# Layer 1 of a four-layer graph network: a second whole weight block, edge passes spread among the moments, column terms moved to GpSimd and ScalarE

## What is computed

```python
h = x @ W;  s1 = h @ a1;  s2 = h @ a2
e = leaky_relu(s1[:, :, None] + s2[:, None, :], 0.2)
att = softmax(where(adj > 0, e, -9e15), axis=1)      # over i, for each column j
x = layernorm(x + elu(att @ h))
```

## Time and profile before

| what | value |
|---|---|
| median of three runs | 418.67 us |
| profiled execution, its own time | 419.3 us |
| its span in the profile | 417.1 us |
| TensorE, weight load, VectorE busy | 362.8, 321.0, 363.4 us |
| ScalarE, GpSimd busy | 307.5, 296.0 us |
| TensorE clock granted, mean | 0.974 of full |

### The profile page before, as it was taken

The page is one execution under the profiler, slowest core; times in us unless marked ns, Lnnn a source line. Parts: engine busy times, 40 slices in busy tenths (PEclk is TensorE's granted clock), DMA queues, the critical chain, the costliest instruction groups (busy, mean ns, idle before and its releaser), DMA issues. The chain is left out here.

```text
span 417.1 us, 9207 instructions
## 1 busy us (share of the span) xinstructions
PE 362.8 (87%) x2786; PEld 321.0 (77%) x2793; DVE 363.4 (87%) x1398; ACT 307.5 (74%) x824; POOL 296.0 (71%) x363
## 2 busy tenths in 40 slices
PE   7898999999969687796896899999998789899980
PEld 7697999999968686796796889899898685455550
DVE  0558899999999999999999988899998997899984
ACT  2757999999766767758858867678786737888862
POOL 5347888777776775664765767777777856899994
PEclk9999999999989999989989999999999989999996
DMA  6999963000000000000000000000000000012222
GB/s 174 217 250 247 244 108 53 2 1 2 2 1 2 1 2 1 2 2 1 2 1 2 2 0 2 2 1 2 0 2 3 0 2 1 2 75 79 75 77 105
DMA packets 8756, 18.20 MB, mean 44 GB/s; under 512 B 1280, under 2 KB 2560, under 8 KB 8704
## 3 DMA queue, kind: packets, MB, share of 16 engines
q0 software_dynamic: 2304, 8.39, 10.6%
q1 hardware_dynamic: 5280, 8.72, 5.9%
q10 hardware_dynamic: 1120, 0.46, 0.5%
HBM read 21.76 MB, written 4.19 MB: 62 GB/s over the span
## 5 line engine op out<-in xcount | busy, mean ns | idle before, releaser
L542 PE MATMUL o_ps<-h_scaled,PT 128*128 128x129 f32 (+1 forms) x1536 | 186.8, 281 | 2.8 <-DVE y L1085 1.2
L542 PEld LDWEIGHTS o_ps<-h_scaled,PT 128*128 128x128 f32 x1536 | 181.4, 197 | 4.8 <-issue 2.5
L1029 DVE SCALAR_TENSOR_TENSOR PT<-rows_ps,factors,MT 128x512 f32<-128x512 f32 x128 | 88.8, 738 | 0.0
L781 ACT ACTIVATE X<-y,rstd 128x128 f32<-128x128 f32 x192 | 61.2, 391 | 28.1 <-POOL rstd L304 28.1
L304 POOL TENSOR_TENSOR rstd<-var_eps,neg_half 128x4 f32<-128x4 f32 x64 | 70.1, 1095 | 5.0
L479 PE MATMUL h_ps<-wx,xT 128*128 128x130 f32 x384 | 53.5, 283 | 20.9 <-DVE smax L978 19.0
L479 PEld LDWEIGHTS h_ps<-wx,xT 128*128 128x128 f32 x384 | 48.4, 194 | 26.6 <-issue 26.4
L1105 DVE BATCH_NORM_STATS2 stats<-y 128x6 f32<-128x128 f32 x256 | 55.9, 281 | 6.5 <-DVE y L1085 0.5
L254 POOL TENSOR_TENSOR mean_term<-h_mean,empty_row 128x512 f32<-128x512 f32 x32 | 38.2, 1194 | 18.7 <-DVE residual L1085 14.1
L319 POOL TENSOR_TENSOR elu_exp<-elu_exp,X 128x512 f32<-128x512 f32 x32 | 40.8, 1275 | 7.8 <-ACT elu_exp L774 7.4
L278 POOL TENSOR_TENSOR h_scaled<-hx,factors 128x516 f32<-128x516 f32 x32 | 35.1, 1097 | 13.5 <-PE o_ps L542 7.9
(11 more groups left out here) (120 smaller groups left out, 650.7 us busy)
## 6 DMA issues: line engine op xcount, KB each, us to landing
MT<-adj_by_j POOLq DMA_DIRECT2D x16, 512.0 KB, 13.0
X<-x SPq DMA_DIRECT2D x16, 256.0 KB, 8.3
out<-X SPq DMA_DIRECT2D x16, 256.0 KB, 2.0
w_rel<-w SPq DMA_DIRECT2D x1, 256.0 KB, 3.5
w_back<-w_by_output ACTq DMA_DIRECT2D x1, 192.0 KB, 3.2
wx<-w_by_input ACTq DMA_DIRECT2D x1, 192.0 KB, 3.6
bias<-b ACTq DMA_DIRECT2D x1, 64.0 KB, 3.0
bias<-b SPq DMA_DIRECT2D x1, 64.0 KB, 5.9
```

Source lines behind the costliest of these rows:

```text
L542: last = pe.matmul(o_ps[it.b][:, ic, first:1 + D], PT[:, it.b, jc, ic * P:(ic + 1) * P], h_scaled[:, it.b, jc, first:1 + D], start=(jc == ...
L781: last = act.activation(X[:, it.g, c, :], y[:, it.b, c, :], ACT.Copy, scale=rstd[:, it.b, c:c + 1])
L1029: dve.scalar_tensor_tensor(out=PT[:, it.b, c, :], in0=rows_ps[:], scalar=factors[:, it.b, 1, c:c + 1], in1=m, op0=ALU.max, op1=ALU.mult, * ...
```

## The change

Of the four blocks two are whole instead of one (`WHOLE = 2`), so GpSimd makes two mask-times-rows passes per item, ScalarE fills two blocks, and VectorE makes two edge passes and two masking passes instead of three and three. BELOW is computed on GpSimd, ABOVE on ScalarE as a ReLU with the maximum as bias, and the column weight on GpSimd, as a sum instead of a maximum. take_max(n+3) stands ahead of the column sums. From slot 17 to slot 29 the edge passes of item n+2 are made in slot n, one between sum and moments and one between moments and aggregate, in place of those of item n+1 at the head of the next slot.

```diff
-WHOLE = 1
+WHOLE = 2
 EDGES = C - WHOLE
# GpSimd
+            def below_max(it):
+                pool.wait_ge(sem("smax"), it.done)
+                if it.g >= 2:
+                    pool.wait_ge(sem("rows_ps"), it.done - 2)
+                pool.tensor_scalar(col_tmp[:, it.b, BELOW, :], hx[:, it.r, :, S1], smax[:, it.b:it.b + 1], LOWEST,
+                                   ALU.subtract, ALU.max).then_inc(sem("below"), 1)
+            def column_weight(it):
+                pool.wait_ge(sem("hinge"), it.of_layer)
+                pool.wait_ge(sem("big_col"), it.of_layer)
+                pool.tensor_tensor(col_tmp[:, it.b, WEIGHT, :], col_tmp[:, it.b, HINGE, :], big_col[:, it.g, :],
+                                   ALU.add).then_inc(sem("col_weight"), 1)
...
+                if at(2) and at(2).l == 1:
+                    below_max(at(2))
                 if at(1) and at(1).l == 1:
                     mask_rows(at(1))
...
                 if at(-2):
                     find_rstd(at(-2))
                 split_bias2(n)
+                if at(2) and at(2).l == 1:
+                    column_weight(at(2))
                 if at(1) and at(1).l == 1:
                     scale_h(at(1))
# ScalarE
+            def above_max(it):
+                act.wait_ge(sem("smax"), it.done)
+                act.activation(col_tmp[:, it.b, ABOVE, :], hx[:, it.r, :, S2], ACT.Relu, bias=smax[:, it.b:it.b + 1])\
+                    .then_inc(sem("above"), 1)
...
                 take_bias2(n)
+                if at(2) and at(2).l == 1:
+                    above_max(at(2))
                 if at(-3) and at(-3).l != 1:
                     take_scaled(at(-3))
                 if at(-2) and at(-2).l == 1:
                     take_scaled(at(-2))
# VectorE
-            def node_terms(it):
...
-            def column_weight(it):
...
+            def edges_with_moments(n):
+                return n - 1 >= G and item(n + 2).l == 1
+            def edges(it, cs):
+                if WHOLE in cs:
+                    dve.wait_ge(sem("rows_taken"), it.of_layer)
+                    dve.wait_ge(sem("col_weight"), it.of_layer)
+                for c in cs:
...
-                if at(1) and at(1).l == 1:
-                    edges(at(1))
-                if at(2) and at(2).l == 1:
-                    node_terms(at(2))
+                if at(1) and at(1).l == 1 and not edges_with_moments(n - 1):
+                    edges(at(1), tuple(range(WHOLE, C)))
...
+                if at(3) and at(1) and at(1).l == 1:
+                    take_max(at(3))
                 if at(1) and at(1).l == 1:
                     column_sums(at(1))
...
-                if at(2) and at(2).l == 1:
-                    column_weight(at(2))
                 if at(1) and at(1).l == 1:
                     column_factors(at(1))
-                if at(3) and at(1) and at(1).l == 1:
-                    take_max(at(3))
                 if at(-1) and at(-1).l == 1:
+                    ahead = edges_with_moments(n)
                     add_elu(at(-1))
+                    if ahead:
+                        edges(at(2), (WHOLE,))
                     finish(at(-1))
+                    if ahead:
+                        edges(at(2), (WHOLE + 1,))
                     aggregate(at(-1))
+                    if ahead:
+                        edges(at(2), tuple(range(WHOLE + 2, C)))
```

## The result

The changed kernel takes 443.38 us, the median of four runs (441.77 to 445.24); the kernel before, run beside it, 418.50. The ratio is 1.059, with a 95% interval of 1.056 to 1.062: 24.9 us slower. The profiled execution took 445.24 us with a span of 443.1, against 419.3 and 417.1.

A forecast was written before the change was run, and what follows sets the result against it. VectorE was taken to bound layer 1; the change would close a loop of waits through ScalarE and GpSimd: 25.6 us over twelve slots less 1.5 at entry and 1.5 at exit, +22.6, so 441 us in the median, range 430 to 447.

The forecast's parts named there:

- the ring with both collisions: Forecast case: layer 1's wait loop, with var_eps and rstd both held by VectorE passes; 9.74 us per slot, 441, chance 0.58.
- The ring: Layer 1, from slot 18: rstd releases ScalarE's scaling, fills and hinge, then GpSimd's column_weight through next rstd; 8.94 us per slot.
- The collisions: Two VectorE weight passes reading mask and edge fall on GpSimd's var_eps and rstd, adding 0.80 us per slot.
- the case that the prediction names for an earlier VectorE: If VectorE's passes come earlier, elu_low on GpSimd holds them first, and the collision stays.
- The loop's twelve slots: Slots 18 to 30 of layer 1: 12 x (8.94 + 0.80 - 7.61) = 25.6 us slower.
- Entry: Slots 15 to 17, ahead of the loop: VectorE's gain less GpSimd's new work, 1.5 us gained, between 0 and 3.6.
- take_max only changes place: VectorE's slot: moving take_max was given no cost in the count from 7.61 to 6.39 us.
- Exit: Slot 30: the last item's scale_h need not follow ScalarE's leg; 1.5 us gained, between 0 and 2.7.
- The sum: Twelve slots, entry and exit together: +22.6 us on the profiled 419.3, giving 441.9, or 441 in the median.
- TensorE at no cost: TensorE's attention pass, even at 5.44 us, ends 4.3 us before the loop's 9.74 are over, so costs nothing.
- VectorE's need of 6.39: VectorE's work per layer 1 slot after the change, down from 7.61 us.
- The rivals: Loop with one collision 436 (0.17), none 432 (0.1), longer loop 446 (0.1), VectorE still bounding 401 or 408 (0.04).

The follow-up runs named there:

- run with the passes later: Changed kernel with five more small VectorE instructions per slot between second and third weight pass, from slot 18 on: 434.21 us, ratio to the kernel before 1.039.
- run with rstd first: Changed kernel with the scaling of X one slot later and GpSimd's var_eps and rstd ahead of elu_low: 417.14 us, ratio to the kernel before 0.996.
- With one whole block: For the 6.85 slot: changed kernel with `WHOLE = 1` and also the scaling of X one slot later: 408.71 us, ratio to the kernel before 0.976.

## Why the prediction was right, and where it was off

The time fell into the range, 2.4 us above the point, and the forecast case came true: the ring with both collisions.

- *The ring.* Predicted 8.94 us without collisions and 9.74 with; measured 8.95 (the run with the passes later) and 9.79 in plain slots. That the hinge's place behind rstd makes it is shown by the run that moved the hinge alone. Single terms were off by little: below_max took 0.28 to its successor for 0.23, column_weight 0.15 for 0.20, the way from rstd's end to column_weight 2.71 for 2.73.
- *The collisions.* Priced at 0.80 per slot from rows 7 and 8, at 12 x 0.8 = 9.6 us; the run that takes them away says 9.2. var_eps and rstd take what the earlier trace rows showed. That they came at all was partly luck: counted from the hinge's start, the prediction puts the first pass at 5.2 or 5.0 and var_eps at 5.17, too close to say which comes first. In slot 19 the pass came at 4.95 (150.87 less 145.92) and var_eps at 5.19, so the pass was ahead by 0.24. It was so in each slot from 19 to 29, and in each the tail of elu_low held the pass for 0.1 first, the case that the prediction names for an earlier VectorE.
- *The loop's twelve slots.* 25.6 predicted, 25.45 measured.
- *Entry.* Here steps of the sum were mis-sized: "I take 1.5 gained" for slots 15 to 17, where 1.06 were lost. Up to the rstd of slot 17 there was a gain: it starts at 134.15, against 135.97 before. That is 1.82 and not VectorE's 3.6, since GpSimd had become the bound: in slot 16 it has no idle in front of var_eps, which waited 1.12 us before the change, and that slot is 0.68 longer. The loss falls between the rstd of slot 17 and that of slot 18, 7.90 us against 5.02. The kernel before, then the changed kernel:

```profile
135.97 1.41 POOL L304 TENSOR_TENSOR rstd<-var_eps,neg_half 128x4 f32<-128x4 f32 x1
```

```profile
134.15 1.42 POOL L319 TENSOR_TENSOR rstd<-var_eps,neg_half 128x4 f32<-128x4 f32 x1
...
135.56 0.20 POOL L310 TENSOR_TENSOR col_tmp<-col_tmp,big_col 128x4 f32<-128x4 f32 x1
...
135.85 0.29 DVE L1004 TENSOR_REDUCE smax<-h_ps 128x1 f32<-128x128 f32 x1 [1.15 <-PE h_ps L526]
...
136.50 1.04 POOL L278 TENSOR_TENSOR h_scaled<-hx,col_tmp 128x512 f32<-128x512 f32 x1 [0.75 <-DVE col_tmp L1064]
...
137.80 2.30 POOL L295 TENSOR_TENSOR edge<-MT,q_rows 128x512 f32<-128x512 bf16 x2
...
141.28 0.70 POOL L316 TENSOR_TENSOR var_eps<-mean_var,eps_tile 128x4 f32<-128x4 f32 x1
```

  Of the 2.88 us, 1.60 are the new work (on record 1.55), 0.49 are var_eps held by a pass, and 0.75 are a wait of scale_h that the prediction had at nothing. "take_max only changes place", it says; but the new place is ahead of the reciprocal (L1064). VectorE's maximum (L1004) waited 1.15 us for TensorE, which was on an attention pass of 5.44 us until 135.27 and on the transposes behind it. The pass had stood behind 1.11 us of idle, at a granted clock of 0.69 on the mean; the same pass took 3.81 at 1.00 before the change. Reciprocal and scale_h waited with the maximum.
- *Exit.* 1.5 predicted, 0.51 measured. scale_h of the last item was indeed freed of the hinge but not of VectorE, where the maximum stands ahead of the reciprocal again and waits 0.64 us for TensorE:

```profile
261.33 0.29 DVE L1004 TENSOR_REDUCE smax<-h_ps 128x1 f32<-128x128 f32 x1 [0.64 <-PE h_ps L526]
...
261.99 1.04 POOL L278 TENSOR_TENSOR h_scaled<-hx,col_tmp 128x512 f32<-128x512 f32 x1 [2.19 <-DVE col_tmp L1064]
```

  Against the earlier trace rows it waits 2.19 instead of 2.69 for the same reciprocal.
- *The sum.* Entry and exit together explain the difference: 22.6 predicted, 26.0 in the profiled executions, of which the median of four runs shows 24.9. Of the 3.4 between 22.6 and 26.0, the two waits behind take_max are 1.4; this is read from the trace, since no run leaves take_max in its old place.
- *TensorE at no cost.* In the loop this held: its granted clock was lower than before, and the slot was still the ring's 9.79. At entry and exit it did not hold, by the two waits above. What such a clock would cost in a shorter ring was not tried.
- *VectorE's need of 6.39.* The run with rstd first bears it out: VectorE has no gap there at 7.30 us a slot, and less the hold of 1.00 that is 6.30. With one whole block it is 6.85.

The rivals fell: the collisions were there in full, the two small GpSimd operations took 0.43 together as on record, and a gain came only in the runs whose slot is below the 7.61 of the kernel before. The two parts of the change do not add up. Two whole blocks alone cost 14.2 us, and the moved terms with the spread edge passes alone gain 6.5, which would leave 7.7; together they cost 24.9. Of the difference 9.2 are collisions, which neither part has in the steady slots by itself. The other 8.0 I put down to VectorE's saved time, which is worth nothing where a ring sets the slot: without collisions the slot is 8.95 with both parts and 8.76 with two whole blocks alone.

## What to carry to other kernels

Where engines run in order and wait for one another, follow each new wait back through what stands ahead of it on the other engine, until it comes home or ends: here a ring of waits set the slot by its sum, though each engine in it was idle part of the time. Moving an instruction of 0.19 us brought the slot from 9.73 to 7.92, so its place in the queue was worth more than its length. Before work is taken off the bounding engine, check that what it is traded for does not lengthen the longest ring. And an instruction that "only changes place" takes its wait along: what stands behind it now waits too.

## What was not expected of the hardware

An rstd does not hold a two-input pass of VectorE that starts inside it: in the run with the passes later, the pass from 158.71 took 0.74 within an rstd from 158.25 to 159.28, and none of the passes that began inside an rstd in slots 18 to 29 of that run took longer than 0.75. An elementwise pass of GpSimd does hold it, for most of what is left of it: in the run with rstd first the pass took 1.75, 1.00 more than a free one, with 1.20 us of elu_low left. The Trainium skill, "SBUF — State Buffer", section "SBUF: two separate sides", says that of two such instructions the one that starts first has the shared port pair to SBUF for its whole instruction. For elu_low the trace agrees to 0.2 us; for rstd it does not, and the measurement decides. Which of the two engines lost was set by a few tenths of a microsecond of order: elu_low 0.14 ahead of the pass held VectorE, and a pass 0.24 ahead of var_eps held GpSimd. Giving VectorE 1.06 us more to do per slot made the kernel 9.2 us faster.
